# Turned feed-forward values copied as 32-bit words, with their offset of 1536 taken off by a one-row matmul

## The reference, cut to what matters

```python
def _bitlinear(x, w):
    rms = rsqrt(maximum(mean(w * w), EPS))
    w_quant = clip(round(w * rms), -1.0, 1.0) / rms
    scale = 127.0 / maximum(max(abs(x), axis=-1, keepdims=True), EPS)
    x_quant = clip(round(x * scale), -128.0, 127.0) / scale
    return einsum('bsd,fd->bsf', x_quant, w_quant)

h = _bitlinear(layernorm(t), w1)      # 512 -> 2048
h = gelu(h)
t = t + _bitlinear(h, w2)             # 2048 -> 512
```

## Time and profile before

| | |
|---|---|
| median of 3 executions | 349.19 us (347.63 to 349.54) |
| the profiled execution's span, first to last instruction | 346.6 us |
| TensorE, busy / matmuls | 299.3 us (86%) / 2230 |
| VectorE, busy / instructions | 280.0 us (81%) / 667 |
| ScalarE, busy / instructions | 223.5 us (64%) / 493 |
| GpSimd, busy / instructions | 140.6 us (41%) / 193 |
| mean granted TensorE clock | 0.979 |

### The profile page before, as it was taken

The page is one execution under the profiler, slowest core; times in us unless marked ns, Lnnn a source line. Parts: engine busy times, 40 slices in busy tenths (PEclk is TensorE's granted clock), DMA queues, the critical chain, the costliest instruction groups (busy, mean ns, idle before and its releaser), DMA issues. The chain is left out here.

```text
span 346.6 us, 7553 instructions
## 1 busy us (share of the span) xinstructions
PE 299.3 (86%) x2230; PEld 177.2 (51%) x2230; DVE 280.0 (81%) x667; ACT 223.5 (64%) x493; POOL 140.6 (41%) x193
## 2 busy tenths in 40 slices
PE   3557765898899999997899999896999999999994
PEld 2345633744555555554564655462555565554452
DVE  1658989888899989885899899949899898989940
ACT  2386495694676767665658676863767676666662
POOL 6406327134443544343333733352235433553340
PEclk9999999699999999999899999998999999999999
DMA  4999300000010401040011201130104010101102
GB/s 123 345 393 396 108 1 2 0 2 3 1 46 2 137 2 48 2 139 2 0 45 44 93 0 46 43 96 0 45 1 136 0 45 1 45 0 48 46 2 91
DMA packets 21446, 22.35 MB, mean 64 GB/s; under 512 B 1384, under 2 KB 18792, under 8 KB 20904
## 3 DMA queue, kind: packets, MB, share of 16 engines
q1 hardware_dynamic: 19752, 20.98, 18.2%
q10 hardware_dynamic: 1664, 1.05, 1.1%
HBM read 15.73 MB, written 6.29 MB: 64 GB/s over the span
## 5 line engine op out<-in xcount | busy, mean ns | idle before, releaser
L1154 PE MATMUL ps_o<-w2T,hq 128*128 128x512 f16 x384 | 93.5, 382 | 0.0
L1131 PE MATMUL ps_h<-w1T,xq 128*128 128x512 f16 x296 | 74.6, 388 | 1.2 <-ACT xq L511 0.7
L463 POOL TENSOR_SCALAR w_room<-w_room,q 128x2048 f32<-128x2048 f32 x24 | 47.4, 1975 | 62.7 <-DVE q L846 62.7
L511 ACT ACTIVATE w_room<-ps_h,s 128x512 f32<-128x512 f32 x74 | 50.3, 688 | 15.6 <-PE ps_h L1131 15.3
L833 DVE TENSOR_REDUCE amax<-w_room 128x1 f32<-128x1024 f32 x48 | 57.1, 1206 | 1.5 <-ACT w_room L511 1.5
L1154 PEld LDWEIGHTS ps_o<-w2T,hq 128*128 128x128 f16 x384 | 35.3, 98 | 37.0 <-ACT hq L511 3.3
L511 ACT ACTIVATE hq<-ps_t 128x512 f16<-128x512 f16 x96 | 51.3, 606 | 2.6 <-PE ps_t L1144 2.5
L1131 PEld LDWEIGHTS ps_h<-w1T,xq 128*128 128x128 f16 x296 | 27.6, 100 | 33.7 <-issue 3.7
L511 ACT ACTIVATE junk_m<-front 128x192 bf16<-128x192 f32 x64 | 20.6, 330 | 34.8 <-DVE pooled L746 34.8
L805 DVE SCALAR_TENSOR_TENSOR t<-pv,sg,xt 128x512 f32<-128x512 f32 x24 | 33.5, 1397 | 5.6 <-issue 2.9
L457 POOL TENSOR_SCALAR cen<-cen,q 128x512 f32<-128x512 f32 x24 | 16.6, 690 | 38.0 <-DVE q L828 38.0
(11 more groups left out here) (126 smaller groups left out, 496.9 us busy)
## 6 DMA issues: line engine op xcount, KB each, us to landing
x_in<-in_x SPq DMA_DIRECT2D x16, 384.0 KB, 4.4
out<-w_room SPq DMA_DIRECT2D x16, 384.0 KB, 2.6
w_room<-in_L_ffn_w SPq DMA_DIRECT2D x4, 1024.0 KB, 8.8
w_raw<-in_L_ffn_w SPq DMA_DIRECT2D x4, 1024.0 KB, 12.0
x_in<-in_x ACTq DMA_DIRECT2D x2, 384.0 KB, 3.9
fc_raw<-in_L_conv_fc_w ACTq DMA_DIRECT2D x2, 128.0 KB, 4.3
taps_rev<-in_L_conv_sa_w SPq DMA_DIRECT2D x2, 0.2 KB
taps_rev<-in_L_conv_sa_w SPq DMA_DIRECT2D x2, 0.3 KB
```

The source lines that it names most:

```text
L463: pool.tensor_scalar(c[:, :], c[:, :], q2[tile.par][:, 0:1], MAGIC, ALU.mult, ALU.add).then_inc(g_rounded, 1)
L511: act.activation(out_ap, in_ap, func, **more).then_inc(signal, 1)
L1131: last = pe.matmul(banks[b], xq[tile.pair.par][:, tile.s, k, :], w1T[:, k, b * 512:(b + 1) * 512], start=(k == 0), stop=(k == NC - 1))
L1154: last = pe.matmul(ps_o[:, :], hq[tile.par][:, k, :], w2T[:, k, :], start=(k == 0), stop=(k == NF - 1))
```

## The change

`copy_hq` has two passes where it had four. Each reads a whole bank of `ps_t` as 512 words of 32 bits and writes them to `hq` as they are, without a bias, so `hq` now holds 1536 + n. A new matmul opens every accumulation of `ffn_out`: one row of -1536 (`shift_row`) times one row with the column sums of `w2T` (`w2_col`). The sums come from 16 matmuls with a column of ones, `sum_w2`, in the hand-written part, and a copy on ACT, `copy_w2_col`. The waits on `hq_ready` count in halves instead of quarters, and `copy_out` in A and B stands between the two passes.

```diff
+        col_ones = sb("col_ones", [P, 1], f16)
+        shift_row = sb("shift_row", [1, P], f16)
+        w2_col = sb("w2_col", [1, C], f16)
...
+        hq_words = [b[:, :, :].rearrange("p k q -> p (k q)").bitcast(f32) for b in hq]
...
             def copy_hq(tile, out_tile=None, out_bank=None):
-                for i in range(4):
-                    wait(act, h_turned, tile.at(2, i // 2 + 1))
-                    copy(hq[tile.par][:, i * NF // 4:(i + 1) * NF // 4, :],
-                         ps_t[i // 2][:, i % 2 * 512:(i % 2 + 1) * 512].rearrange("p (k q) -> p k q", q=P),
-                         hq_ready, bias=-F16_ZERO)
-                    if i == 1 and out_tile:
+                for i in range(2):
+                    wait(act, h_turned, tile.at(2, i + 1))
+                    copy(hq_words[tile.par][:, i * 512:(i + 1) * 512], ps_t[i][:, :].bitcast(f32), hq_ready)
+                    if i == 0 and out_tile:
                         copy_out(out_tile, out_bank)
+
+            def copy_w2_col():
+                act.wait_ge(w2_summed, 1)
+                copy(w2_col[:, :], ps_o[0:1, :], w2_col_ready)
...
             gelu(Tile(pair0, 1), None, h_start, (2, 3))
+            copy_w2_col()
             copy_hq(Tile(pair0, 0))
...
+            dve.memset(col_ones[:, :], 1.0).then_inc(masks_ready, 1)
+            dve.memset(shift_row[:, :], -F16_ZERO).then_inc(masks_ready, 1)
...
                 for i in range(2):
-                    wait(pe, hq_ready, tile.at(4, 2 * i - 2))
+                    wait(pe, hq_ready, tile.at(2, i - 1))
...
             def ffn_out(tile, quarters):
                 for i in quarters:
-                    wait(pe, hq_ready, tile.at(4, i + 1))
+                    wait(pe, hq_ready, tile.at(2, i // 2 + 1))
                     if i == 0:
                         wait(pe, res_ready, tile.at(1, 0))
+                        pe.wait_ge(w2_col_ready, 1)
+                        pe.matmul(ps_o[:, :], shift_row[:, :], w2_col[:, :], start=True, stop=False)
                     for k in range(i * NF // 4, (i + 1) * NF // 4):
                         last = pe.matmul(ps_o[:, :], hq[tile.par][:, k, :], w2T[:, k, :],
-                                         start=(k == 0), stop=(k == NF - 1))
+                                         start=False, stop=(k == NF - 1))
...
+            def sum_w2():
+
+                pe.wait_ge(masks_ready, 4)
+                for k in range(NF):
+                    last = pe.matmul(ps_o[0:1, :], col_ones[:, :], w2T[:, k, :], start=(k == 0), stop=(k == NF - 1))
+                last.then_inc(w2_summed, 1)
...
             weights_ready(1)
+            sum_w2()
             turn_hq(Tile(pair0, 0))
```

More of the change, by code:

```diff
@@ L233, in metaformer_kernel @@
         hq_ready = sem("hq_ready")
+        w2_summed = sem("w2_summed")
+        w2_col_ready = sem("w2_col_ready")
         o_done = sem("o_done")
```

## The result

| | before | after |
|---|---|---|
| median | 349.37 us (4 executions, 347.63 to 350.30) | 354.58 us (4 executions, 352.96 to 355.73) |
| ratio | | 1.015 (95% interval 1.010 to 1.020) |
| the same kernel measured again, beside experiments 2 to 4 | 348.89 us (17) | 353.32 us (5), ratio 1.012 (1.010 to 1.014) |
| span of the profiled execution | 346.6 us | 353.8 us |

The change makes the kernel slower by 1.2 to 1.5%, 4 to 5 us. The forecast was +3.7 us and 352.9 us. The page of the changed kernel answers to the earlier trace rows: busy time by engine, then the group of `copy_hq`.

The account below looks back on a forecast made before the run. DVE was taken to set the loop's pace, though PE is busier. ACT's relief 0, column sums 2.0, loop matmuls 1.0 and end 0.7 gave +3.7 us on 349.2: 352.9 us, range 349.6 to 356.6.

Parts of the forecast that it names:

- Rival 2: Loop: PE sets the pace, so every new matmul costs 0.40 us; 360.8 us in all, chance 0.08.
- Rival 1: Behind `copy_hq` in tile C: DVE waits for ACT, so a pair gains up to 0.97 us; 346.1 us, chance 0.08.
- rival 3: `copy_hq`: 32-bit passes take as long as 1024 16-bit values, so two passes come late; 355.5 us, chance 0.07.
- one wait near a microsecond: Loop: DVE goes from instruction to instruction with only this wait in the 35.14 us between two sums behind a convolution.
- the pair at 0.96: Loop pair of 38.0 us at granted clock 0.96: its extra 3 us were put down to DVE's issue gaps.
- The matmul per tile: New one-row matmul in `ffn_out`: 0.40 us between full ones, together 1.0 us in the loop, bounds 0 and 2.8.
- A and C: Loop tiles where the new matmul costs nothing: 0.40 us before a room of 0.49, and 0.22 before 0.31.
- The term for B: Tile B, before `fc1`: 0.05 us in each of 5 pairs, 0.40 in two with a loop start; together 1.0 us.
- The column sums: Hand-written part: `turn_hq` 3.25 us later, plus 0.40 for the new matmul, less 1.59; DVE late by 2.0 us.
- that wait was worth 1.59: Hand-written part: PE's wait for POOL's `cen` until 79.92 us absorbs 1.59 us of the added work.
- the wait for `cen` moves along: Hand-written part: upper bound of the column sums, where that wait absorbs nothing; 3.6 us.
- The end: Last tile, from `turn_hq` through the last `ffn_out` and `turn_res`: 0.7 us more, bounds 0.4 and 1.0.

Follow-up runs that it names:

- experiment 2: Changed kernel without column sums and one-row matmul, so only two-pass word copies and the two memsets: ratio 1.002 to the kernel before, +0.8 us.
- experiment 3: Changed kernel without the one-row matmul per tile; word copies and column sums stay: 351.57 us, ratio 1.008 to the kernel before.
- experiment 4: Changed kernel without column sums, its row of sums set to zero; word copies and one-row matmul stay: 352.12 us, ratio 1.010 to the kernel before.
- experiment 6: Kernel before with two-pass word copies alone, no memsets, column sums or one-row matmul, DVE's stream untouched: ratio 1.002 to the kernel before, +0.9 us.
- experiment 10: Changed kernel with memsets on GpSimd, correction over 128 full rows, and column sums in four parts between blocks of `ffn_in`: 352.04 us, ratio 1.006.
- experiment 7: Changed kernel with two further one-row matmuls of zeros per tile and one more small memset: 360.25 us, 11.6 over the kernel before.
- experiment 11: Kernel before with six small memsets more at the start of DVE's stream: ratio 1.001 to the kernel before, +0.5 us.
- experiment 8: Changed kernel with the correction spread over 128 full rows, so every weight tile is full: 353.46 us, ratio 1.013 to the kernel before.
- experiment 9: Changed kernel with its two memsets moved from DVE to GpSimd: 353.87 us, ratio 1.012 to the kernel before.
- experiment 5: Kernel before with only the change's two small memsets added on DVE: ratio 1.005 to the kernel before, +1.9 us.
- experiment 1: The changed kernel measured again with no edit: ratio 1.012 to the kernel before, +4.4 us.

## Why the prediction was right, and what in it was not

**The direction and the range** were right: 354.58 and 353.32 us against 352.9, within 349.6 to 356.6, and slower beyond the interval. The size was a little low, +3.7 against +4.4 and +5.2, and that it came so near is partly luck. By the medians the parts are 0.8 for the words with the two memsets (0 forecast), 1.9 for the sums (2.0) and 2.4 for the matmul per tile with the end (1.7), 5.1 in all. The 1.9 is an average over executions in which the sums cost about 1.4 and about 3, and for the 0.8 no cause was found.

**What bounds the kernel.** Right, and shown for the pairs without a loop start: there the pace is DVE's. 20 us less on ScalarE moved nothing (experiment 6), and with full rows PE's extra matmul cost nothing (experiment 10). With twice as much more it showed (experiment 7), as rooms of 0.3 to 0.5 us would have it. Rival 2 (nothing is hidden) had 0.40 per tile; it was 0.10. Rival 1 (faster through ScalarE's queue) is out, and so is rival 3: a pass is 592 ns. DVE's stream isn't quite alone, though: the "one wait near a microsecond" is for GpSimd, and it is the same in the changed kernel, so GpSimd's `rs` belongs to the chain that sets the pace.

```profile
198.14 0.21 DVE L822 TENSOR_SCALAR lim<-amax,rs 128x1 f32<-128x1 f32 x1 [0.93 <-POOL rs L430]
```

One reading under it was wrong: that the clock doesn't count because the pair at 0.96 is explained by DVE's idle time. The two stretches named for it, 2.88 and 1.51 us, make 4.4 us and not the 2.9 by which the pair is longer. And the second pair with a loop start took 38.67 us before and 37.87 in experiment 6 at clock 1.00, with the same DVE stream, and 39.50 and 38.29 us in experiments 2 and 3, which is 0.8 and 1.2 us for the clock. In none of the pairs with a loop start that ran at 1.00 (experiments 3, 6, 10 and 11) does DVE wait for `fc1`; at 0.96 it waits 0.4 to 1.4 us in all but two. The size isn't sharp: the first such pair took 38.00 and 38.35 us in the kernel before and experiment 6, both with a stretch of low clock.

**The matmul per tile.** The 0.40 us, with about 0.1 on either side for the change of shape, is shown by experiment 8: 0.32 to the next start with one row, 0.22 with full rows. A and C took it in. In B the room was read right: in the second halves `fc1` was ready 0.41 us before DVE took it up, and with the one-row matmul DVE takes it up 0.04 behind, 0.05 us later than it would. The term for B, 1.0 us in the loop, was 1.16 in experiment 4. But its parts were off: I had 0.05 for a pair without a loop start and 0.4 for one with. The 0.4 came in DVE's wait for `fc1` (experiment 4), not in the length of the pair each time. Against equal DVE streams the second halves show 0.1 (35.14 to 35.24, experiment 9). In the changed kernel's own stream it was 0.3, since DVE there had lost an idle stretch of 0.25 us with the memsets and, held up 0.05 by `fc1`, has one of 0.2 beside it again. This is the stretch in the changed kernel; that the delay brought it back is only likely:

```profile
217.62 0.15 DVE L762 TENSOR_SCALAR hid_r<-small 64x4 f32<-64x4 f32 x1
217.80 0.15 DVE L763 TENSOR_TENSOR hid<-hid_r 64x2 f32<-64x2 f32 x1
218.11 0.21 DVE L848 TENSOR_SCALAR lim<-amax 128x1 f32<-128x1 f32 x1 [0.15 <-issue]
```

**The column sums.** This is the term that was mis-sized: 2.0 us forecast, 4.1 in the first profile. The step that failed is the start of the sums, "when the last `ffn_in` has issued, 74.02 + 4 x 0.216 = 74.88", together with "that wait was worth 1.59": both are of an execution whose clock had risen at 69.6 us. In nine of the thirteen profiles it rose at 73.8 to 74.9. Then `ffn_in` ends up to 2 us later, and of the wait for `cen` 0.27 us are left before any sums come (experiment 2). The same step gave 1.8 to 2.0 where the clock had risen by 68.5 (experiment 7) and 3.4 where it hadn't (3). The late rise isn't the change's doing. It is there without the sums (experiments 2, 4, 6 and 11) and missing with them (7 and 8), and the nine profiles that have it already had the lower clock from 12.4 to 13.5 us on, which the other four had not. In the executions' medians, which mix both, the sums cost 1.9. My bounds, 1.7 to 3.6, held these but for the first profile, and "the wait for `cen` moves along" at their upper end was the right number for another reason.

**The end.** 0.7 forecast, 0.6 and 0.75 measured.

**The two memsets** I had costed at nothing, as lying in DVE's first wait. Their time does lie there. But they move DVE's idle stretches, and in the kernel before the whole was 1.9 us longer with them (experiment 5). That these 1.9 us come from the moved stretches isn't shown: by the profile the difference lies in the pairs with a loop start (+1.5 each), the same two memsets beside word copies cost nothing (experiment 2 against 6), and taking them out of the changed kernel won nothing that can be told (9). What makes the pairs with a loop start so much longer in experiment 5 remains open.

## What to carry to other kernels

Find the engine whose instructions keep their distances, not the one with the most busy time. Here work taken from another engine was worth nothing, and work given to one with small waits was free until the waits in its way were used up. Price a wait that is to absorb new work at both levels of the clock, since one execution's profile shows only one, and a slow clock may need the same room. And where a change touches an engine at the start only, compare the loop with and without that alone: here two tiny instructions moved idle stretches in every later pair.

## What the runs showed of the hardware

- A matmul of 512 columns with weights of 1 or 6 rows next to one with full weights costs about 0.1 us more at each change: 0.31 to 0.32 from the start of the one to that of the other, 0.22 with full weights (experiments 1 and 8). So does a change to weights of one column: 0.31 into the column sums and out of them, 0.216 between them (experiment 1). One row is not faster by itself: 0.38 to 0.39 us alone in both forms.
- DVE has idle stretches of 0.2 to 0.4 us in its steady stream that nothing it waits for explains. They recur at the same instruction in all three second halves, and two instructions more at the program's start move them (35.07 and 35.14 us per pair to 35.47 and 34.92; experiments 5 and 6). What is behind them wasn't tried.
- The granted clock differed from execution to execution: its mean in the executions of the kernel before alone lay between 0.916 and 0.984. In the profiles, one execution each, the stretch at 1.2 GHz that begins at 60 to 64 us ended at 68.4 to 69.6 us in four and at 73.8 to 74.9 in nine, with the column sums and without them.
